# The second layer's bias matmul with 128 rows of contraction in place of 3

## The reference

```python
gate_A = sigmoid(ifft(gA_f * x_f)); gate_B = sigmoid(ifft(gB_f * x_f))   # 7x7 circular convolutions
a_t = a_spatial * gate_A;  b_t = ifft(B_f * x_f) * gate_B
# a scan of T=8 equal steps in log space over a_t and b_t, then
h_final = exp(log_h[-1])
return h_final @ W_out + b_out                                           # then x + this
```

## Time and profile before

| | us |
|---|---|
| runs of the kernel before | 6893.54, 6856.88, 6883.95 (median 6883.95) |
| the profiled execution, its time | 6909.09 |
| its span, first to last instruction | 6907.3 |
| PE matmul busy | 5912.3 (86%) |
| DVE, ACT, POOL busy | 4477.4 (65%), 3641.9 (53%), 4068.1 (59%) |
| mean granted PE clock, as a share of full speed | 0.942 |

### The profile page before, as it was taken

One profiled execution on the slowest core, in us unless ns is written; L12 is line 12 of the kernel. 1 busy time (PEld: TensorE's weight loads), 2 busy tenths in 40 slices (PEclk: granted clock), 3 DMA queues, 4 the chain that ended last, 5 costly groups with the idle time before them and its releaser, 6 DMA issues. The chain is left out here.

```text
span 6907.3 us, 144255 instructions
## 1 busy us (share of the span) xinstructions
PE 5912.3 (86%) x51796; PEld 5278.5 (76%) x51796; DVE 4477.4 (65%) x5283; ACT 3641.9 (53%) x4872; POOL 4068.1 (59%) x3608
## 2 busy tenths in 40 slices
PE   6799999999999999999871378888888888888898
PEld 5678888888888888888761277777777777777787
DVE  6367777777777777777744556666666666666652
ACT  5655556555555555555421355555555555555552
POOL 0146666666666666666671676676666666666640
PEclk8899999999999999999985699999999999999996
DMA  5356667666677666676561589999999899999985
GB/s 129 122 166 208 198 207 216 198 205 201 202 211 209 203 202 201 204 216 205 169 176 50 148 218 247 243 255 249 257 244 255 241 255 255 244 249 250 251 231 154
DMA packets 1239334, 1441.35 MB, mean 209 GB/s; under 512 B 142960, under 2 KB 1025396, under 8 KB 1238516
## 3 DMA queue, kind: packets, MB, share of 16 engines
q1 hardware_dynamic: 1238516, 1431.07, 73.4%
HBM read 999.09 MB, written 431.64 MB: 207 GB/s over the span
## 5 line engine op out<-in xcount | busy, mean ns | idle before, releaser
L1283 PE MATMUL psC<-wide,xhl 128*128 128x256 bf16 x6144 | 1042.9, 280 | 198.6 <-DVE xhl L1451 170.4
L1220 POOL TENSOR_TENSOR stage<-stage,nrow 128x1024 f32<-128x1024 f32 x256 | 652.3, 2549 | 597.7 <-DMA stage<-x_by_block_row 583.0
L1280 PE MATMUL psC<-wide,xhl 128*128 128x192 bf16 x6144 | 868.6, 251 | 0.0
L1237 POOL COPY down<-xhl 48x448 f32<-48x448 f32 x512 | 522.5, 1021 | 545.6 <-PE psC L1289 486.4
L812 POOL TENSOR_TENSOR y<-y,grow 128x1024 f32<-128x1024 f32 x256 | 604.0, 2359 | 323.7 <-DVE y L656 323.7
L1283 PEld LDWEIGHTS psC<-wide,xhl 128*128 128x128 bf16 x6144 | 593.6, 115 | 210.0 <-issue 195.1
L1456 DVE SCALAR_TENSOR_TENSOR xhl<-xhl,psC 128x512 f32<-128x512 f32 x512 | 348.9, 682 | 540.4 <-ACT xhl L1372 539.9
L1387 ACT ACTIVATE hT<-psH 128x512 f32<-128x512 f32 x512 | 305.2, 596 | 700.0 <-PE psH L1325 699.7
L823 POOL TENSOR_TENSOR q<-q,qinv 128x1024 f32<-128x1024 f32 x256 | 490.1, 1914 | 309.4 <-DVE qinv L730 309.4
L1372 ACT ACTIVATE xhl<-psC 128x512 f32<-128x512 f32 x512 | 304.8, 599 | 664.0 <-PE psC L1289 662.5
L1289 PE MATMUL psC<-narrow,down 128*128 128x96 bf16 x6144 | 532.5, 211 | 143.0 <-DMA narrow<-toeplitz_narrow 94.9
(11 more groups left out here) (166 smaller groups left out, 14383.7 us busy)
## 6 DMA issues: line engine op xcount, KB each, us to landing
wide<-toeplitz_wide SPq DMA_DIRECT2D x1024, 140.0 KB, 4.3
xa<-in_x SPq DMA_DIRECT2D x256, 512.0 KB, 4.6
xb<-in_x SPq DMA_DIRECT2D x256, 512.0 KB, 3.8
xc<-in_x SPq DMA_DIRECT2D x256, 512.0 KB, 5.7
x_rows<-xc SPq DMA_DIRECT2D x256, 512.0 KB
res<-x_rows SPq DMA_DIRECT2D x256, 512.0 KB, 7.4
out<-res SPq DMA_DIRECT2D x256, 512.0 KB, 6.4
stage<-x_by_block_row SPq DMA_DIRECT2D x240, 512.0 KB, 7.1
```

The source lines that it names most:

```text
L1220: nc.gpsimd.tensor_tensor(v, v, nrow[:, 0:1, :].to_broadcast([P, NP_, C]), ALU.mult).then_inc(s_scaled, 1)
L1237: nc.gpsimd.tensor_copy(dst[lo, :, :, 0:last], src[lo, :, 0:NQ, CW:])
L1280: nc.tensor.matmul(dst[:, :, :, 2:], lhs, tab[:, :, 32 + part * 12:44 + part * 12], start=False, stop=False)
L1283: nc.tensor.matmul(dst, lhs, tab[:, :, part * 16:part * 16 + 16], start=(n == 0), stop=False)
```

## The change

`bias_k` and `ones3` get 128 rows instead of 3. A fifth memset on DVE fills all of `bias_k` with zeros before the three bias rows are copied into it, `ones3` is filled with ones in all 128 rows, and the two waits for `s_chain` count 9. The matmul then contracts over 128 rows of which 125 are zero in the moving operand; the sum is the same.

```diff
-        bias_k = sb("bias_k", [3, 1, C], BF16)
-        ones3 = sb("ones3", [3, P], BF16)
+        bias_k = sb("bias_k", [P, 1, C], BF16)
+        ones3 = sb("ones3", [P, P], BF16)
...
-            sp.wait_ge(s_chain, 8)
+            sp.wait_ge(s_chain, 9)
             for i in range(3):
                 sp.dma_start(bias_k[i:i + 1, 0, :], bias3[:, i, :]).then_inc(s_bias_k, 16)
...
-            pe.wait_ge(s_chain, 8)
+            pe.wait_ge(s_chain, 9)
...
                 nc.tensor.matmul(psO[:].rearrange("p (s c) -> p s c", c=C), ones3[:],
-                                 bias_k[:].to_broadcast([3, HS, C]), start=True, stop=False)
+                                 bias_k[:].to_broadcast([P, HS, C]), start=True, stop=False)
...
             t_.then(nc.vector.memset(ones3[:], 1.0))
+            t_.then(nc.vector.memset(bias_k[:], 0.0))
```

## The result

The changed kernel takes 6820.97 us (median of 6 runs, 6817.88 to 6843.83) against 6881.04 us for the kernel before (median of 6, 6856.88 to 6893.54): a ratio of 0.9927, 95% interval 0.9909 to 0.9945. It is faster by 60 us. The direction was right and the time lies inside the stated range, but the forecast was a gain of 123 us.

A forecast was written before the change was run, and what follows sets the result against it. PE was taken to bound image 15 and the last pass; in the slower middle PE waits for DVE, POOL for loads. 65 + 13 + 9 + 36 = 123 us off 6884 gave 6760; stated range 6690 to 6840.

The forecast's parts named there:

- The stall: Around the 3-row bias matmul: 0.31 us lost, taken as 0.29, because of few rows; 128 rows expected to behave like 96.
- Rival 3: At the bias matmul: the stall is not due to rows, nothing gained, 6884 to 6897 us; chance 0.08.
- The middle: Images 1 to 14: half of 9.3 us of PE time per image reaches the end, 65 us; ends 0 and 130.
- rival 2: Images 1 to 14: POOL's floor and the loads absorb the saving, only the ends remain, 6839 to 6860 us; chance 0.09.
- The clock in the middle: Images 1 to 14: fewer stretches at half speed if added rows count as work, 13 us; ends -10 and 40.
- Image 15: Last image, no next image to load: PE is the limit, so 9.3 us saved; ends 5 and 9.3.
- The last pass: After the last convolution: stalls go and clock rises to 1.00, cycles 2.1 to 2.3 us, 36 us; ends 15 and 40.
- rival 1: The last pass stays at the low clock: 15 us there in place of 36, 6781 us; chance 0.15.
- The forecast's own range: Whole kernel: 6700 to 6830 us, the middle and its clock giving 20 us at one end, 140 at the other.
- my signs of being wrong: Distances around the bias matmul stay, the middle keeps 183 us, or POOL's wait for stage loads grows by over 100 us.
- The slower rival: PE ahead makes wide tables collide with stage loads, delaying POOL, DVE and the addition; 47 us slower, 6931; chance 0.05.
- The new memset: At the start, on DVE ahead of SP's bias copies: filling `bias_k` costs 0.2 us, all of which counts.

The follow-up runs named there:

- light tables: Wide tables' four DMAs per block cut to one table row each: 6732.0 us (0.9774) on the changed kernel, 6828.8 us (0.9921) on the kernel before.
- narrow first: 128 rows with the late shift, each block's narrow table issued ahead of the four wide DMAs in SP's queue: 6790.6 us (0.9856).
- late shift: DVE's shift of the next image's stage moved one slot later: 6784.6 us (0.9849) on the changed kernel, 6810.5 us (0.9886) on the kernel before.
- the two edits after it: Each on 128 rows with the late shift: narrow first, 6790.6 us; POOL's scaling of a stage one slot later too, 6788.7 us.

## Why the prediction was right and wrong

- **The stall: right.** 0.32 to 0.22 and 1.00 to 0.89 behind the bias, 0.10 ahead gone, as the first layer's 96-row matmul said. The number of rows is the cause, shown by 64 against 96. Rival 3 is out. The Trainium skill's rule on weight loads, which spoke against the change ("TensorE: Matmul & The Clock Gate", "Part 3: Packing small matmuls"), does not agree with these traces: loads of full-row matmuls start ahead of them here too, 0.04 us at the bias.
- **The middle: the failed step.** "I take half: 14 x 4.65 = 65 us" and 13 for the clock; 26 came, 0.2 of the 130 us. I took half from PE's 35% of the chain. That share did not tell what a step of PE's work is worth: after the change its five lines still have 31%, and taking 67 to 85 us more away saved nothing. DMA's 0.92 stood in the same rows, and I gave it no part in the sum. With light tables the same edit passes 5.0 of 9.3 us per image, just the half I took; with full tables 1.9. The 44 us between (37 by the medians) are the loads'. That is rival 2, to which I gave 0.09, in part rather than in full.
- **The clock in the middle: nothing gained.** I took 13 us, with an end of -10. It went from 0.97 to 0.96, and stands at 0.97 with 96 rows.
- **Image 15: 3 us for 9.3.** PE busy fell by 7.6 us, the stage by 3; PE was 95% busy and was taken as its own limit, which it is not quite. It is 156 with light tables as well, so not the loads. The clock goes with it: with one bias matmul of 96 or 128 rows the image took 155 or 156 us in six profiles with a clock of 0.98, and 152, my forecast, in the one with 1.00 (narrow first); with 3 rows it took 159 at 0.98 to 1.00. So at 1.00, one profile against one, 7 of the 9.3 us come. Why the image mostly has 0.98 stays open.
- **The last pass: 41 us for 36.** The cycle was given as 2.1 to 2.3 and is 2.14, with `psO` as the new limit. The clock rose as I took it, but that was luck in part, as my reason, a 96-row bias among such matmuls in the first layer, is not needed. The stage's clock is also 0.91 without the bias matmul, hence without the added rows, and with 64 rows, hence with the stalls; there the stage takes 94 us, so of the 41 us the clock gave some 35 and the stalls 6. Even the 3 rows with the late shift had it for half the pass:

```profile
6730.00:6750.00 20.00, 19.87 (x77) 14.99 (x76) 4.82 (x10) 3.58 (x6) 0.00 (x0) 0.50 0.56 153
6750.00:6770.00 20.00, 17.77 (x103) 14.05 (x103) 5.14 (x8) 4.18 (x7) 0.00 (x0) 0.83 0.71 192
6770.00:6790.00 20.00, 16.08 (x110) 12.56 (x110) 5.92 (x9) 5.37 (x9) 0.00 (x0) 1.00 0.82 228
```

  PE was busy 19.87 of the 20 us at 0.50 ahead of that rise. Of the other three 3-row profiles the kernel before had 0.50 to the end of the pass, and the two with light tables 0.50 until its last 26 and 24 us, which have 0.63 and 0.78 (0.51, 0.54 and 0.56 over the stage). What tips it stays open. The Trainium skill's rule on transposes behind rival 1 ("TensorE: Matmul & The Clock Gate", "Part 4: PE-mode transpose") is not borne out: a third of this pass's f32 matmuls are transposes, and all nine kernels with 64 rows or more and the one without a bias went to the full clock (0.89 to 0.92 over this stage, which begins with a stretch of idle).
- **The range and the signs.** The forecast's own range ends at 6830, but its terms, 20 + 9 + 36, make 6819, and with 15 for the last pass 6840. That 6821 lies inside the stated range is owed to the low end of the middle and to a last pass that gave 5 us more than its term, not to the half. None of my signs of being wrong came up: the distances changed, the middle went from 183.6 to 181.8, and POOL's wait grew by 20 us, not 100. They were too wide to catch a middle with a third of its forecast.
- **The slower rival** named the right chain, faster PE to later loads to a later addition, and loads did land later, but by 0.2 and 0.4 us, not by the 1.45 it needed.
- **The new memset** took 0.11 us for the 0.2 forecast; the start of the layer moved by 5 us between the two executions, and among all of them by up to 18 with no pattern, so nothing can be read from it.
- The rows ahead of the prediction hold; one sentence there counts the split of the bias wrongly: three of its five instructions count on `s_chain`, which with the four memsets and the addition makes 8. In the prediction, the span of 6907.3 is 23 us over the median, not 25.

## What to carry to other kernels

Between full-size matmuls, give a small one 96 to 128 rows, with zeros where there is nothing: in this kernel the 3 rows cost some 0.3 us more than the 128. But before a saving on an engine is carried to the end, ask what else is nearly full. Here others waited mostly for PE and it had 35% of the chain, and still 26 of 130 us passed with the DMA engines at 92% busy, against 70 at 70%. A pair of kernels with that resource lightened, with and without the change, tells at once how much it takes. And an edit that removes a wait beside a nearly full resource may show it again elsewhere: the late shift turned 153 us less waiting for the addition into 178 us more for narrow tables, and the two edits after it each cut a wait by over 150 us for no time at all.

## What the runs showed of the hardware that was not expected

- A matmul of 3 or of 64 rows between full ones costs 0.10 us ahead and 0.20 behind at the full clock, at 96 and 128 rows nothing. In the last pass at 1.2 GHz the cost is 0.47 us per half row, by 3.46 against the 2.99 worked out from the earlier trace rows.
- The same load of 168 KB takes 2.9 us to land at a DMA share of 0.71, 5.1 at 0.92 and 7.4 at 0.95, while the rate over the whole stage rises only from 250 to 256 GB/s between the last two. At 0.96 it took 6.8 or 7.5.
- In the last pass PE was 98% busy at a clock of 0.50 before the change, and idle for a fifth of each cycle (0.44 of 2.14 us) at 1.00 after it.
